# Two attentions with heads of 64 take the row sums of two steps from all exponentials, and the heads-of-16 attention interleaves the scores of two pairs and brings its q/k chunk forward

## The reference, cut to what matters

```python
# block 0 (block 3 also normalises q and k per head)
q, k, v = jnp.split(qkv, 3, axis=-1)              # 16 heads of 64
attn = jnp.einsum('bqhd,bkhd->bhqk', q, k) * scale
attn = jax.nn.softmax(attn, axis=-1)
out = jnp.einsum('bhqk,bkhd->bqhd', attn, v).reshape(Bq, Tq, INNER)
return out @ W_out + b_out
...
# block 2: 16 heads of 16, with a mask over the keys
scores = jnp.where(mask, jnp.einsum('bhnd,bhmd->bhnm', q, k) * scale, -jnp.inf)
out = jnp.einsum('bhnm,bhmd->bhnd', jax.nn.softmax(scores, axis=-1), v)
```

## Time and profile before

| | us |
|---|---|
| median of 3 runs | 3338.05 |
| the 3 runs | 3335.65, 3338.05, 3476.47 |
| the profiled execution, its own time | 3335.07 |
| its span, first to last instruction | 3333.3 |

### The profile page before, as it was taken

The page is one execution under the profiler, slowest core; times in us unless marked ns, Lnnn a source line. Parts: engine busy times, 40 slices in busy tenths (PEclk is TensorE's granted clock), DMA queues, the critical chain, the costliest instruction groups (busy, mean ns, idle before and its releaser), DMA issues. The chain is left out here.

```text
span 3333.3 us, 70757 instructions
## 1 busy us (share of the span) xinstructions
PE 3028.1 (91%) x26089; PEld 2516.2 (75%) x26090; DVE 2154.0 (65%) x4193; ACT 1694.8 (51%) x3085; POOL 915.1 (27%) x725
## 2 busy tenths in 40 slices
PE   7999999997998989999999699799999999994697
PEld 5887888775998979877777598577777777772586
DVE  4655565655666766567777566757575757567775
ACT  3444444443554445554455345566666666662364
POOL 2232323232112231122222211322222222221574
PEclk8999999998999999999999799899999999997799
DMA  5000000001001000000000100100000000004243
GB/s 171 4 6 6 6 3 6 6 6 36 19 19 46 0 23 0 22 4 9 9 9 9 46 19 19 36 1 0 0 0 0 0 0 0 0 1 130 80 126 86
DMA packets 68976, 80.66 MB, mean 24 GB/s; under 512 B 10146, under 2 KB 61090, under 8 KB 68884
## 3 DMA queue, kind: packets, MB, share of 16 engines
q1 hardware_dynamic: 62756, 71.14, 7.4%
q0 software_dynamic: 6144, 8.52, 1.4%
HBM read 66.80 MB, written 12.85 MB: 24 GB/s over the span
## 5 line engine op out<-in xcount | busy, mean ns | idle before, releaser
L956 POOL TENSOR_TENSOR L3a_shift<-L3a_neg,L3a_mx 128x256 fp32r<-128x256 f32 x128 | 94.7, 740 | 523.1 <-DVE L3a_mx L1556 523.1
L1063 ACT ACTIVATE L0a_prob<-L0a_st 128x512 f32<-128x512 f32 x256 | 134.0, 602 | 160.4 <-PE L0a_st L1293 72.6
L945 POOL TENSOR_TENSOR L0a_o<-L0a_prob 128x1024 f32<-128x1024 f32 x48 | 118.8, 2475 | 302.6 <-PE L0a_o L1330 302.6
L1063 ACT ACTIVATE L3a_prob<-L3a_st 128x512 f32<-128x512 f32 x256 | 133.8, 602 | 117.8 <-POOL L3a_o L945 90.0
L1925 ACT ACTIVATE L2a_prob<-L2a_st 128x512 f32<-128x512 f32 x256 | 132.2, 604 | 117.7 <-PE L2a_st L1958 117.7
L1556 DVE TENSOR_REDUCE L0a_mx<-L0a_s 128x2 f32<-128x512 f32 x224 | 143.8, 683 | 73.9 <-PE L0a_s L1267 73.9
L1546 DVE SCALAR_TENSOR_TENSOR L3a_qk_lo<-raw,cols_sb,L3a_qk_hi 128x256 fp32r<-128x256 f32 x256 | 157.9, 656 | 36.5 <-ACT L3a_qk_hi L1054 36.5
L1556 DVE TENSOR_REDUCE L3a_mx<-L3a_s 128x2 f32<-128x512 f32 x256 | 163.7, 679 | 15.5 <-PE L3a_s L1267 15.5
L2190 DVE TENSOR_REDUCE L2a_mx<-L2a_s 128x2 fp32r<-128x512 f32 x256 | 163.5, 681 | 15.2 <-PE L2a_s L1958 15.2
L1157 PE MATMUL L0a_st<-L0a_xt,home 128*128 128x256 f32 x512 | 150.1, 293 | 5.1 <-DVE home L1664 5.1
L1158 PE MATMUL L0a_st<-L0a_xt,home 128*128 128x256 f32 x512 | 145.6, 284 | 0.0
(11 more groups left out here) (615 smaller groups left out, 11241.6 us busy)
## 6 DMA issues: line engine op xcount, KB each, us to landing
raw<-in_moe_w SPq DMA_DIRECT2D x16, 1024.0 KB, 8.6
x_sb<-in_x SPq DMA_DIRECT2D x1, 4096.0 KB, 24.9
L0a_gate<-gate_rows SPq DMA_DIRECT2D x32, 128.0 KB, 3.9
L0m_gate<-gate_rows SPq DMA_DIRECT2D x32, 128.0 KB, 3.8
L2a_gates<-gate_rows SPq DMA_DIRECT2D x32, 128.0 KB, 3.9
L2m_gate<-gate_rows SPq DMA_DIRECT2D x32, 128.0 KB, 3.8
out_x<-x_sb SPq DMA_DIRECT2D x1, 4096.0 KB, 17.0
token_rows<-x_sb SPq DMA_DIRECT2D x1, 4096.0 KB, 29.3
```

The costliest lines, as they stand in the source:

```text
L945: nc.gpsimd.tensor_tensor(half_sums, both[:, :, :, 0:N], both[:, :, :, N:2 * N], ALU.add).then_inc(halves_done, 1)
L956: nc.gpsimd.tensor_tensor(shift[:, u % 4, :, :, :], neg64[:].unsqueeze(1).unsqueeze(1).to_broadcast([P, 2, TT, 64]), mx[:, u % 2, :, :].un ...
L1063: A(prob[:, u % 4, h, :], st_ps[u % 2][h][:], ACT.Exp, scale=64 ** -0.5).then_inc(p_done, 1)
```

## The change

In `heads64`, `sums(0)` and `sums(1)` use all exponentials instead of POOL's halves, and stand right behind `column_part(0)` and `column_part(1)`. POOL keeps only `halves(2)`, and ACT's two waits for `halves` go. In `heads16`, PE's `scores_t` takes both pairs in turn, two heads of the one and two of the other, but for slot 1 of all batches except the last, where the wait for `x_low` stays between the pairs; in slot 3 the wait for `taken` now stands ahead of both pairs. In slot 1, `over` moves on PE behind `qk` and `max_rows`. On DVE, `x_low` moves from the end of slot 0 to between the two maxima that begin slot 1, `over` moves behind `shift` and `qk_low`, and `o_low` 0 and 1 go to slot 2. On ACT, `o_high(0)` moves behind `qk_high`.

```diff
@@ -959,10 +959,8 @@
                 def body(i):
                     for u in range(6):
                         shift_of(i, u)
-                    halves(i, 0)
                     shift_of(i, 6)
                     shift_of(i, 7)
-                    halves(i, 1)
                     halves(i, 2)
 
                 token_rstd(1)
@@ -982,8 +980,7 @@
                     if not first:
                         for n in range(PAIRS):
                             o_low(i - 1, n)
-                    for p in range(3):
-                        halves(i, p)
+                    halves(i, 2)
                     tail(i)
 
                 token_rstd(1)
@@ -1098,8 +1095,6 @@
                 for p in range(PAIRS + 1):
                     if p == 1 and not final:
                         act.wait_ge(xlo_done, i + 2)
-                    if p in (2, 3):
-                        act.wait_ge(halves_done, 3 * i + p - 1)
                     if p < PAIRS:
                         exp(2 * p, 0)
                         exp(2 * p, 1)
@@ -1335,7 +1330,7 @@
                 def sums(p, halved):
 
                     if halved:
-                        pe.wait_ge(halves_done, 3 * i + p + 1)
+                        pe.wait_ge(halves_done, i + 1)
                     else:
                         pe.wait_ge(p_done, 2 * (U * i + 2 * p) + 4)
                     for kt in range(1 if halved else TT):
@@ -1344,7 +1339,7 @@
                                 at = 64 * odd + 32 * h
                                 last = mm(sum_ps[at:at + 32, 0:N], sum_sel[:, p, :],
                                           half_sums[:, odd, h, :] if halved else prob[:, (2 * p + odd) % 4, h, kt * N:(kt + 1) * N],
-                                          start=(p == 0), stop=(p == 2), skip_group_check=True)
+                                          start=(p == 0 and kt == 0), stop=(p == 2), skip_group_check=True)
                     if p == 2:
                         last.then_inc(sums_done, 1)
 
@@ -1422,9 +1417,9 @@
                 values(3)
                 for p in range(1, PAIRS):
                     row_part(p)
-                    if p >= 2:
-                        sums(p - 2, True)
                     column_part(p - 1)
+                    if p < 3:
+                        sums(p - 1, False)
                 if not final:
                     pe.wait_ge(xlo_done, i + 2)
                     pe.wait_ge(p_done, 2 * (U * i + 6) + 1)
@@ -1928,13 +1923,12 @@
                         A(v[:, :, :, 0:16], v_ps[:].rearrange("p (t h d) -> p t h d", t=TT, d=16), ACT.Copy).then_inc(v_done, 1)
                         if not first:
                             row_high(i - 1)
-                    if u == 1 and not first:
-                        o_high(i - 1, 0)
                     if u == 0 or not final:
                         qk_high(U * i + u + 3, (u + 3) % U, 0)
                     if u == 0 and not final:
                         x_hi(i + 1)
                     if u == 1 and not first:
+                        o_high(i - 1, 0)
                         o_high(i - 1, 1)
                     if u % 2:
                         act.wait_ge(pv_done, PIECES * i + u // 2 + 1)
@@ -2026,15 +2020,16 @@
                 last.then_inc(mxt_done, 1)
 
             def body(i, first, final):
-                def scores_t(w):
+                def scores_t(u, pairs):
                     for kt in range(TT):
                         ks = slice(N + kt * P, N + (kt + 1) * P)
                         for n, (a, b) in enumerate(((qk_hi, qk_hi), (qk_lo, qk_hi), (qk_hi, qk_lo))):
-                            for h in range(2):
-                                last = mm(st_ps[w % 2][h][:, kt * N:(kt + 1) * N], a[rows(w, h), w // 2, ks], b[rows(w, h), w // 2, 0:N],
-                                          start=(kt == 0 and n == 0), stop=(n == 2))
-                                if kt == TT - 1 and n == 2:
-                                    last.then_inc(st_done, 1)
+                            for w in pairs:
+                                for h in range(2):
+                                    last = mm(st_ps[w][h][:, kt * N:(kt + 1) * N], a[rows(w, h), u, ks], b[rows(w, h), u, 0:N],
+                                              start=(kt == 0 and n == 0), stop=(n == 2))
+                                    if kt == TT - 1 and n == 2:
+                                        last.then_inc(st_done, 1)
 
                 def values():
                     for tt in range(TT):
@@ -2061,12 +2056,14 @@
                         pe.wait_ge(v_done, i + 1)
                     if u == 2 and not first:
                         pe.wait_ge(on_done, PIECES * i)
-                    scores_t(2 * u)
                     if u == 1 and not final:
+                        scores_t(u, (0,))
                         pe.wait_ge(xlo_done, i + 2)
-                    if u == 3 and not first:
-                        pe.wait_ge(taken, i)
-                    scores_t(2 * u + 1)
+                        scores_t(u, (1,))
+                    else:
+                        if u == 3 and not first:
+                            pe.wait_ge(taken, i)
+                        scores_t(u, (0, 1))
                     if u == 0 and not first:
                         gather_sums(i - 1)
                     if ahead:
@@ -2075,10 +2072,6 @@
                     if u == 0:
                         pe.wait_ge(p_done, 4 * slot + 2)
                         values()
-                    if u == 1 and not first:
-                        pe.wait_ge(p_done, 4 * slot + 3)
-                        over(i - 1, 0)
-                        over(i - 1, 1)
                     if u == 0 or not final:
                         pe.wait_ge(p_done, 4 * slot + 1)
                         if u == 1:
@@ -2089,6 +2082,10 @@
                         if u == 1 and not first:
                             pe.wait_ge(rsum_done, i)
                         max_rows(u + 1)
+                    if u == 1 and not first:
+                        pe.wait_ge(p_done, 4 * slot + 3)
+                        over(i - 1, 0)
+                        over(i - 1, 1)
                     if beyond:
                         pe.wait_ge(qkhi_done, slot + 3)
                         scores(2 * slot + 4, 2 * u + 4)
@@ -2182,9 +2179,9 @@
                 dve.wait_ge(qkhi_done, chunk + 1)
                 V.tensor_tensor(qk_lo[:, c, :], ring[bank][:], qk_hi[:, c, :].bitcast(F32), ALU.subtract).then_inc(qklo_done, 1)
 
-            def maxes(pair, w):
-
-                for h in range(2):
+            def maxes(pair, w, heads=(0, 1)):
+
+                for h in heads:
                     dve.wait_ge(s_done, 2 * pair + h + 1)
                     at = 64 * (w % 2) + 32 * h
                     V.tensor_reduce(mx[:, w // 2 % 2, :, at], s_ps[h][:].rearrange("p (t n) -> p t n", t=TT), AX.X, ALU.max).then_inc(mx_done, 1)
@@ -2199,29 +2196,31 @@
                 for u in range(U):
                     slot = U * i + u
                     ahead = not final or u < U - 1
-                    if ahead:
+                    if ahead and u == 1 and not final:
+                        maxes(2 * slot + 2, 2 * u + 2, (0,))
+                        x_low(i + 1)
+                        maxes(2 * slot + 2, 2 * u + 2, (1,))
+                    elif ahead:
                         maxes(2 * slot + 2, 2 * u + 2)
                     if u == 0 and not first:
                         reciprocals(i - 1)
                     if u == 2 and not first:
-                        o_low(i - 1, 1)
+                        o_low(i - 1, 0)
                     if u == 3 and not first:
                         moments(i - 1)
                     if ahead:
                         maxes(2 * slot + 3, 2 * u + 3)
                     if u == 0 and not first:
                         row_low(i - 1)
+                    if u == 2 and not first:
+                        o_low(i - 1, 1)
+                    if ahead:
+                        shift(slot + 1, (u + 1) % U)
+                    if u == 0 or not final:
+                        qk_low(U * i + u + 3, (u + 3) % U, 0)
                     if u == 1 and not first:
                         over(i - 1, 0)
                         over(i - 1, 1)
-                    if ahead:
-                        shift(slot + 1, (u + 1) % U)
-                    if u == 1 and not first:
-                        o_low(i - 1, 0)
-                    if u == 0 or not final:
-                        qk_low(U * i + u + 3, (u + 3) % U, 0)
-                    if u == 0 and not final:
-                        x_low(i + 1)
                     if u == 2 and not first:
                         take(i - 1)
                     if final:
```

## The result

The changed kernel takes 3294.65 us (median of four runs, 3292.74 to 3300.73), the kernel before 3336.85 beside it: a ratio of 0.9878 (95% interval 0.9859 to 0.9897). In a second set of runs it was 3295.73 us, ratio 0.9877 (0.9861 to 0.9894). The forecast was 3297, inside its range, and "within 2%". The profiled execution is 3294.88 us, its span 3293.1, 40.2 us shorter than before. Single runs far above the others of their kernel (3476 of before; 11288, 7028 and 6519 of three experiments) count in the medians but not in the ratios.

The account below looks back on a forecast made before the run. PE, busy 91% of the span, was taken to set the pace. L0a +0.6, L3a -20.0 and L2a -18.6 us sum to -38.0, so 3335.1 becomes 3297 us; range 3284 to 3319, the likeliest's own 3285 to 3308.

Parts of the forecast that it names:

- Part 1: Row sums in L0a on all exponentials: sums(0) wins or loses nothing, 0.04 us more per batch, +0.6 us.
- free only POOL: L0a: POOL's two dropped additions free only POOL, which is idle most of the time.
- Part 2: Row sums in L3a: the stretch to column_part(2) becomes as long as L0a's, -1.25 us per batch, -20.0 us.
- even with the long `qn_low`: L3a: no stall comes back; DVE would finish the second qn_low near 2556.5, and PE needs it near 2556.6.
- Part 3: Two pairs interleaved in L2a: second pair done 0.34 us sooner, but only slot 0 gains, 0.1 us.
- Rival A: L2a's interleaved sets: PE cannot be fed, 62.5 ns per matmul being the pace of issue; 3331 us, chance 0.07.
- rival D: L2a's interleaved sets: each change between pairs restarts the array, set lasts 2.6 us; +82 us, 3379 us, chance 0.04.
- Part 4: L2a's slot 1 falls from 7.4 to 6.2 us, -1.2 us; the new last wait, on over's products, only just covered.
- The chunk at 1.75: L2a, slot 1: the q/k chunk comes 1.75 us after the slot's start, needing only the first exponential, done at about 1.65.
- -0.4 us for both: L2a's first and last batches together gain only 0.4 us, against 1.3 us for each of the 14 in the middle.

## Why the prediction was right, and where it was not

*What bounds the kernel.* PE's gaps set everything, as said: PE's busy time fell by 2.6 us, with 513 matmuls more, and the span by 40.2.

*Part 1, L0a, +0.04 per batch.* Measured +0.01, inside the rounding. Missing was the last batch, which I never looked at: it alone has weight work on DVE, POOL's `halves` slowed it, and the 4.23 us won there are more than L3a gives in three batches. I had written that the two dropped additions "free only POOL"; that sentence was wrong. The rows that should have warned me stood in the prediction itself, `qn_low` at 2.15 against 1.22 beside `halves`: the same effect had to be looked for wherever DVE works beside POOL.

*Part 2, L3a, -1.25.* Measured -1.36. The stretch came out as long as L0a's, 10.63 against 10.62 us (402.44 to 413.06), which was the argument. I had taken 0.04 off for the longer sums, which L0a does not show (0.01); the other 0.07 is probably PE's restart after the wait of 0.45, which goes with it, since a first row after a wait is longer (0.39 against 0.28); no run separates it. DVE's slowing, named there as what makes DVE late, costs 0.13 us in the new order by the run with spare additions. That the new order would hold "even with the long `qn_low`" was forecast, and is borne out; how much of the old loss was the slowing stays open.

*Part 3, interleaving.* 0.1 per batch, in slot 0 alone, forecast; 0.11 and 0.12 measured in two ways. Rival A (the pace of issue, 62.5 ns per matmul) and rival D (a restart at each change of pair) are out: 24 matmuls start within 0.69 us, and the next work 0.22 us later.

*Part 4, slot 1.* 6.29 against a forecast of 6.2, and the batch -1.27 against -1.3. The products of `over` are the last wait, as said, but not quite covered: in each of the 14 batches in the middle slot 2 starts 0.15 us after they end, 0.16 later than `weighted` alone would let it. The chunk at 1.75 rested on both moves, and the prediction did not price them apart: 28.65, 27.96 and 27.50 show that `x_low`'s is worth nothing without `over`'s, and 0.46 us with it.

*The failed step* is "the first has no `over`, the last no `qk` in slot 1 and so nothing to lay over the maxima: -0.4 us for both". The first batch, from its first scores to the next batch's row sums, took 26.70 us before and 27.22 and 26.00 in the two profiles of the changed kernel, so no gain can be told there; the last lost 3.97. I had seen that nothing lies over the maxima there and did not ask what then waits: DVE's weight work, which is in no other batch, stands ahead of the maxima, the moved `over` left a bare wait of 1.38 us behind the one of 1.58, and the clock fell to half. Another 1.5 us went the other way, again by luck: in the profile of before, one batch in the middle took 30.32 instead of 28.77 at a clock of 0.66 (1650 to 1655 us), and after there was none.

Over all profiled runs, 7 of the 56 distances ahead of the last are 1.5 us longer where `over` stands at its old place (none in the kernel with interleaving alone, four in the one with L3a's sums alone), and none of 140 where it stands at its new one. That slot 1's gaps make the clock fall there is likely, not shown; why it falls in one batch and not in the next, with the same waits, is open. For the last batch it is shown that the early weight work is needed for the loss: with that work later the batch is shorter than before the change, wherever `over` stands (28.64 and 28.71). What the later work would give the kernel before was not run. With the early work, the new place of `over` goes with the longer batches, but one profile with the old place took as long, so its share stays open; how much of the 3.97 is the waits themselves and how much the half clock was not measured apart either.

## What to carry to other kernels

Read the first and the last batch of each phase by themselves: the last carries the weights of the next phase, either can lack the work that covers a wait, and here two last batches moved 4 us each, as much as three batches in the middle. When an engine is relieved of an operation, look at what the other engines do beside it (here DVE beside POOL) and not only at those that wait for it. One of two moves can be worth nothing until the other is made, so judge such edits together as well as apart. And look at a second profile before a clock is put down to a wait.

## What was not expected of the hardware

- A DVE subtraction with SBUF operands of 128x1024 took 3.41 or 3.42 us instead of 1.22 when POOL began to add 128x1024 (2.52 us) just ahead of it, in each of the four kernels looked at that have an addition there, and ended 1.08 or 1.09 us after it; a reduction out of PSUM beside such an addition kept its 1.29 us for two.
- The same waits of PE do not give the same granted clock. Behind waits of 1.58 and 1.38 us with 0.5 us of work between them it was 0.50 for 15 us in one execution of the changed kernel, although PE was busy 4.25 us of the first 5, and 0.73, 0.84 and 0.50 in the three windows of another. With the longer stretch of `over` between waits of 1.23 and 0.23, it was still 0.94 in the five us behind them before the change, and 0.66 (1860 to 1865 us) in the kernel with L3a's sums alone.
- Matmuls on four row groups of 32 start four at a time, 0.12 us apart, when the two pairs are issued in turn. Issued one after the other, the second pair starts 0.36 us after the first (1626.63, 1626.99), ahead of the last three of the first pair's six steps, and shares two of them. A change between row groups costs nothing that these rows show.
